# A decoder layer's linear attention: denominators turned to reciprocals on a folded tile and spread by DMA

## What is computed

```
qkv = x @ w_qkv
q_proj = _elu1(jnp.einsum('bhnd,hdf->bhnf', q, proj_matrix))
k_proj = _elu1(jnp.einsum('bhnd,hdf->bhnf', k, proj_matrix))
kv = jnp.einsum('bhnf,bhnd->bhfd', k_proj, v)
attn = jnp.einsum('bhnf,bhfd->bhnd', q_proj, kv)
k_sum = k_proj.sum(axis=2)
z = 1.0 / (jnp.einsum('bhnf,bhf->bhn', q_proj, k_sum) + 1e-08)
attn = attn * z[..., None]
return out @ w_out + b_out      # out: attn with its heads side by side
```

## Time and profile before

| | us |
|---|---|
| median of 3 runs | 2382.08 |
| all three | 2378.66, 2382.08, 2383.08 |
| the profiled execution | 2380.94 |
| its span, first to last instruction | 2379.2 |
| TensorE busy in the span | 2278.0 (96%) |
| VectorE busy | 1390.5 (58%) |
| ScalarE busy | 1158.5 (49%) |
| GpSimd busy | 838.9 (35%) |

### The profile page before, as it was taken

The page is one execution under the profiler, slowest core; times in us unless marked ns, Lnnn a source line. Parts: engine busy times, 40 slices in busy tenths (PEclk is TensorE's granted clock), DMA queues, the critical chain, the costliest instruction groups (busy, mean ns, idle before and its releaser), DMA issues.

```text
span 2379.2 us, 34267 instructions
## 1 busy us (share of the span) xinstructions
PE 2278.0 (96%) x12200; PEld 1775.7 (75%) x12200; DVE 1390.5 (58%) x2258; ACT 1158.5 (49%) x2745; POOL 838.9 (35%) x820
## 2 busy tenths in 40 slices
PE   7999999899998899998799999999999999999998
PEld 6888886566666566665588878888788887888887
DVE  5555456777774668777644466444664445644444
ACT  3555566767663767774544444333343333433332
POOL 1444345333341245545677762111111111111111
PEclk9999999999999899999899999999999999999999
DMA  7655546666646457784656546454345543464442
GB/s 209 161 146 128 134 107 157 210 187 195 177 142 181 102 145 188 185 225 138 217 174 212 177 141 214 171 177 142 129 153 201 177 142 125 136 215 139 140 139 77
DMA packets 140218, 387.46 MB, mean 163 GB/s; under 512 B 15920, under 2 KB 38064, under 8 KB 123440
## 3 DMA queue, kind: packets, MB, share of 16 engines
q1 hardware_dynamic: 139760, 384.77, 53.9%
q10 hardware_dynamic: 288, 0.49, 0.1%
HBM read 254.00 MB, written 104.07 MB: 151 GB/s over the span
## 4 chain that ended last, share of the span: by engine, by line
PE 51%; DVE 1%; issue 0%; ACT 0%; DVEq 0%
PE ex_pg L2593 32%; PE ex_pd L2609 18%; DVE ex_xb L2410 0%; PE ex_pd L2559 0%; PE ex_pd L2570 0%; DVE ex_up L2430 0%; DVE ex_acc L2447 0%; ACT ex_xb L2260 0%; DVE stage L2406 0%; DVE ex_ht L2439 0%; DVE ex_lg L2348 0%; DVE ex_rank L2382 0%; DVE ex_gt L2379 0%; DVE ex_rank L2380 0%; DVE ex_g L2423 0%
## 5 line engine op out<-in xcount | busy, mean ns | idle before, releaser
L2593 PE MATMUL ex_pg<-ex_xb,first_wg 128*128 128x512 f32 x3360 | 821.5, 391 | 12.0 <-DVE ex_up L2430 7.0
L2593 PEld LDWEIGHTS ex_pg<-ex_xb,first_wg 128*128 128x128 f32 x3360 | 632.0, 189 | 153.0 <-issue 15.7
L2609 PE MATMUL ex_pd<-ex_wd,ex_ht 128*128 128x512 f32 x1920 | 486.4, 389 | 2.9 <-issue 2.6
L2609 PEld LDWEIGHTS ex_pd<-ex_wd,ex_ht 128*128 128x128 f32 x1920 | 360.0, 188 | 79.1 <-issue 4.5
L2447 DVE SCALAR_TENSOR_TENSOR ex_acc<-ex_pd,ex_share,ex_acc 128x512 f32<-128x512 f32 x320 | 239.7, 749 | 302.4 <-PE ex_pd L2609 302.2
L2267 ACT COPY ex_m<-ex_pg 128x512 f32<-128x512 f32 x240 | 141.1, 588 | 383.5 <-PE ex_pg L2593 383.4
L2211 POOL TENSOR_TENSOR ex_h<-ex_g,ex_up 128x512 f32<-128x512 f32 x80 | 103.3, 1292 | 553.3 <-issue 458.2
L1590 ACT ACTIVATE cr_prob<-cr_s_bank,cr_top 128x154 f32<-128x154 f32 x512 | 194.7, 401 | 89.3 <-DVE cr_top L1700 86.6
L422 POOL TENSOR_TENSOR pr_ks_sum<-pr_ks_sum,pr_kp 128x512 f32<-128x512 f32 x128 | 165.2, 1291 | 161.6 <-DVE pr_kp L570 150.0
L2271 ACT ACTIVATE ex_g<-ex_g 128x512 f32<-128x512 f32 x160 | 101.3, 633 | 238.0 <-DVE ex_g L2423 165.5
L2203 POOL TENSOR_TENSOR ex_wd<-stage,ex_wd 128x512 fp32r<-128x512 f32 x80 | 105.8, 1343 | 260.1 <-ACT ex_wd L2248 260.1
(11 more groups left out here) (222 smaller groups left out, 3588.9 us busy)
## 6 DMA issues: line engine op xcount, KB each, us to landing
first_wg<-w_scratch SPq DMA_DIRECT2D x60, 1024.0 KB, 5.1
first_wg<-w_scratch SPq DMA_DIRECT2D x60, 768.0 KB, 4.3
w_scratch<-first_wg SPq DMA_DIRECT2D x20, 1792.0 KB, 6.8
stage<-in_units SPq DMA_DIRECT2D x60, 512.0 KB, 6.9
qk<-pr_kq SPq DMA_DIRECT2D x192, 128.0 KB, 2.4
qk<-q_scratch SPq DMA_DIRECT2D x96, 256.0 KB, 4.7
cr_q<-xq_scratch SPq DMA_DIRECT2D x96, 256.0 KB, 8.0
q_scratch<-pr_kq SPq DMA_DIRECT2D x128, 128.0 KB, 2.3
```

The costliest lines, as they stand in the source:

```text
L2593: mm = nc.tensor.matmul(pg[f][BANK[j]][:], wg[:, f, j, s, c * P:(c + 1) * P], xb[:, j, m, c * TB:(c + 1) * TB], start=(k == 0 and j in FRESH),
L2609: mm = nc.tensor.matmul(bank_of("D", n, i)[:], ht[:, s, f, k, t * P:(t + 1) * P], wd[:, n % 2, m, f * D:(f + 1) * D], start=(at == 0), sto ...
```

## The change

The spreading by TensorE goes, with its constant, its banks, the split of the reciprocals on ScalarE and GpSimd. Instead SyncE stores the 16 rows of den to DRAM in four DMAs, loads them back as a tile of 128x64, VectorE takes one reciprocal of that, SyncE stores it back and loads it in four broadcasts to a tile rec of 128x4x512 in fp32, and VectorE multiplies from there. `fold_sums` stands first in SyncE's slot 0, `spread_rec` first in slot 1, each with its waits; the query stores follow in slots 1 to 4 (before: 1, 2, 3 and 7). The fourth group of queries moves from slot 6 to 3, the product from slot 2 to 3, and the output tiles from slots 3 to 5 to slots 4 to 6, with the work that hangs on them. DRAM scratch for the rows is doubled, so that the cross stage has its own. In the cross stage GpSimd waits for the last query stores before it clears two tiles.

The diff, cut to its core:

```
     PLAN = {
         0: [("ND", 3), ("XQ", 0, 0, 12)],
         1: [("XQ", 1, 0, 12)],
-        2: [("R", 0), ("R", 1), ("R", 2), ("R", 3), ("XQ", 2, 0, 12)],
-        3: [("ND", 0), ("O", 0, 0, 12)],
-        4: [("O", 1, 0, 12), ("O", 2, 0, 6)],
-        5: [("ND", 1), ("O", 2, 6, 12), ("O", 3, 0, 12)],
-        6: [("XQ", 3, 0, 12), ("T", 0), ("T", 1)],
+        2: [("XQ", 2, 0, 12)],
+        3: [("ND", 0), ("XQ", 3, 0, 12)],
+        4: [("O", 0, 0, 12), ("O", 1, 0, 6)],
+        5: [("ND", 1), ("O", 1, 6, 12), ("O", 2, 0, 12)],
+        6: [("O", 3, 0, 12), ("T", 0), ("T", 1)],
         7: [("ND", 2), ("T", 2), ("T", 3)],
...
-        spread = sb("spread", [P, G, P], F32R)
-        rec = sb("rec", [P, 2, TB], F32R)
+        rec = sb("rec", [P, G, TB])
...
+        ROWS = 96
+        FOLD = H * TB // P
+        folded = [den[:, 1, n * FOLD:(n + 1) * FOLD] for n in range(2)]
+
+        def folded_rows(i):
+            return rec_dram[i].rearrange("h (k n) -> (h k) n", n=FOLD)
+
+        TAKEN = {"XQ": xq_taken, "O": o_taken, "T": turn_lo}
...
+                def fold_sums(i):
+
+                    sp.wait_ge(den_set, i + 1)
+                    for j in range(HG):
+                        sp.dma_start(rec_dram[i, j * G:(j + 1) * G], den[j * HD:j * HD + G, 0]).then_inc(row_out, 16)
+                    sp.wait_ge(row_out, ROWS * i + 64)
+                    sp.dma_start(folded[0], folded_rows(i)).then_inc(row_out, 16)
+
+                def spread_rec(i):
+
+                    sp.wait_ge(recip_set, i + 1)
+                    sp.dma_start(folded_rows(i), folded[1]).then_inc(row_out, 16)
+                    sp.wait_ge(row_out, ROWS * (i + 1))
+                    if i:
+                        sp.wait_ge(divided, G * i)
+                    rows = rec_dram[i].rearrange("(j g) t -> j g t", j=HG)
+                    for j in range(HG):
+                        sp.dma_start(rec[j * HD:(j + 1) * HD], rows[j:j + 1].broadcast_to([HD, G, TB])).then_inc(rec_in, 16)
+
                 def slot(i, s, ahead, now, behind):
-                    if behind and s in (1, 2, 3, 7):
-                        query_out(i - 1, (1, 2, 3, 7).index(s))
+                    if now and s == 0:
+                        fold_sums(i)
+                    if now and s == 1:
+                        spread_rec(i)
+                    if behind and s in (1, 2, 3, 4):
+                        query_out(i - 1, s - 1)
...
-                def reciprocal_low(i, n):
-                    cols = slice(n * TB // 2, (n + 1) * TB // 2)
-                    pool.wait_ge(rec_hi, 2 * i + n + 1)
-                    nc.gpsimd.tensor_tensor(rec[:, LO, cols], den[:, 1, cols], rec[:, HI, cols].bitcast(F32),
-                                            ALU.subtract).then_inc(rec_set, 1)
...
                     if i:
-                        act.wait_ge(rec_set, 2 * i)
+                        act.wait_ge(row_out, ROWS * (i - 1) + 64)
                     nc.scalar.activation(den[:, 0], p_den[:], ACT.Identity, bias=tiny[:]).then_inc(den_set, 1)
...
-                def reciprocal_high(i, n):
-                    cols = slice(n * TB // 2, (n + 1) * TB // 2)
-                    act.wait_ge(recip_set, 2 * i + n + 1)
-                    nc.scalar.copy(rec[:, HI, cols], den[:, 1, cols]).then_inc(rec_hi, 1)
 
                 def normalised(i, g):
                     if g == 0:
                         act.wait_ge(o_full, TT * i) if i else None
-                    act.wait_ge(r_taken, G * i + g + 1)
+                    act.wait_ge(divided, G * i + g + 1)
                     nc.scalar.copy(u_att[:, HI, g], num[:, g]).then_inc(norm_hi, 1)
...
-                    if now and s == 0:
-                        reciprocal_high(i, 0)
                     if behind and s == 0:
                         query(i - 1, 0)
-                    if now and s == 1 and not ahead:
-                        reciprocal_high(i, 1)
                     if behind and s == 1:
                         query(i - 1, 1)
-                    if now and s == 2:
+                    if behind and s == 2:
+                        query(i - 1, 2)
+                    if behind and s == 3:
+                        query(i - 1, 3)
+                    if now and s == 3:
                         for g in range(G):
                             normalised(i, g)
-                    if behind and s == 2:
-                        query(i - 1, 2)
                     if (ahead or i == -1) and s in (3, 5):
                         take_num(i + 1, (s - 3) // 2)
-                    if behind and s == 6:
-                        query(i - 1, 3)
                     if now and s == 6:
                         turned(i, 0)
...
-                def reciprocal(i, n):
-                    cols = slice(n * TB // 2, (n + 1) * TB // 2)
-                    dve.wait_ge(den_set, i + 1)
-                    nc.vector.reciprocal(den[:, 1, cols], den[:, 0, cols]).then_inc(recip_set, 1)
+                def reciprocal(i):
+                    dve.wait_ge(row_out, ROWS * i + 80)
+                    nc.vector.reciprocal(folded[1], folded[0]).then_inc(recip_set, 1)
 
                 def normalise(i, g):
                     dve.wait_ge(num_taken, G * i + g + 1)
-                    dve.wait_ge(r_full, G * i + g + 1)
-                    nc.vector.tensor_tensor(num[:, g], num[:, g], bank_of(i, "R", g)[:], ALU.mult).then_inc(r_taken, 1)
+                    dve.wait_ge(rec_in, 16 * HG * (i + 1))
+                    nc.vector.tensor_tensor(num[:, g], num[:, g], rec[:, g], ALU.mult).then_inc(divided, 1)
...
-                    if s == 1 and now:
-                        reciprocal(i, 1)
+                        dve.wait_ge(const_in, 32)
                     if s == 6 and now:
-                        add_out(i, 3)
+                        add_out(i, 2)
                     if s == 2 and behind:
                         query(i - 1, 1)
-                    if s == 2 and now:
-                        normalise(i, 0)
                     first()
                     if s == 1 and behind:
                         query(i - 1, 0)
                     if s == 3 and behind:
                         query(i - 1, 2)
-                    if s == 0 and now:
-                        reciprocal(i, 0)
-                    if s == 2 and now:
+                    if s == 3 and now:
+                        normalise(i, 0)
                         normalise(i, 1)
+                    if s == 4 and behind:
+                        query(i - 1, 3)
+                    if s == 6 and now:
+                        norm(i, 1)
+                    if s == 1 and now:
+                        reciprocal(i)
+                    second()
+                    if s == 3 and now:
                         normalise(i, 2)
+                        normalise(i, 3)
                     if s == 4 and now:
                         add_out(i, 0)
+                    if s == 5 and now:
+                        add_out(i, 1)
+                        norm(i, 0)
                     if s == 6 and now:
                         norm(i, 2)
...
-                    if s == 6 and behind:
-                        query(i - 1, 3)
-                    second()
-                    if s == 2 and now:
-                        normalise(i, 3)
-                    if s == 6 and now:
-                        norm(i, 3)
...
-                    if s in (4, 5) and now:
-                        add_out(i, s - 3)
-                        norm(i, s - 4)
-                    if s in (6, 7) and now:
-                        turned(i, 2 * s - 12)
-                        turned(i, 2 * s - 11)
+                    if s == 6 and now:
+                        add_out(i, 3)
+                        turned(i, 0)
+                        turned(i, 1)
+                        norm(i, 3)
+                    if s == 7 and now:
+                        turned(i, 2)
+                        turned(i, 3)
...
-                def spread_out(i, g):
-                    bank_free((i, "R", g))
-                    if g == 0:
-                        pe.wait_ge(rec_set, 2 * (i + 1))
-                    for s in (HI, LO):
-                        mm = nc.tensor.matmul(bank_of(i, "R", g)[:], spread[:, g], rec[:, s], start=(s == HI),
-                                              stop=(s == LO))
-                    mm.then_inc(r_full, 1)
...
+                for landed in xq_out:
+                    pool.wait_ge(landed, 16 * NB * BLK * G // 2)
```

More of the change, by code:

```diff
@@ L106, in decoder_kernel @@
     x1_dram = nc.dram_tensor("x1_scratch", [NBLK, P, TT * D], F32).ap()
-    rec_dram = nc.dram_tensor("rec_scratch", [NBLK, H, TB], F32).ap()
+    rec_dram = nc.dram_tensor("rec_scratch", [2, NBLK, H, TB], F32).ap()
     xq_dram = nc.dram_tensor("xq_scratch", [NBLK, 2, P, C * TB], F32).ap()
@@ L162, in decoder_kernel @@
```

(22 more changed lines are left out.)

16 lines of the change are left out of this document (4 added, 12 removed).

## The result

The changed kernel takes 2474.32 us (median of 4 runs, 2470.6 to 2476.36), the kernel before 2380.85 (4 runs, 2378.66 to 2383.08): a ratio of 1.0391, 95% interval 1.0373 to 1.0409. It is 93 us slower. Forecast were 2473 us, a range of 2403 to 2505, and a chance of 0.88 for slower.

What follows compares the result with a forecast made beforehand. TensorE, the only full engine, bounds the kernel. Middle block -3.1 + 11.5 + 1.1 + 1.3 = +10.8 us, 65 in six; blocks 1, 0, 7 add 8, 5, 14; all +92 on 2382, about 2473 us, range 2403 to 2505.

Steps and rivals of the forecast that it cites:

- Rows landed: Linear stage, each block: the four row stores land at t = 8.5 us, behind the load of x.
- Fold, reciprocal, store back, spread: Rest of a block's DRAM round trip: 2.0, 0.5, 1.6 and 7.5 us, reciprocals in SBUF at t = 20.1.
- The query store: On SyncE's queue it lies behind the spread and lands at t = 21.7 us; ScalarE's query 2 waits for it.
- rival A: Query store doesn't wait for the spread, only the product is late: +4.5 to +5 us a block, 2425 us; chance 0.22.
- From there to slot 5: From the query store's landing, through query, product, cast, subtractions and output matmuls, to slot 5: 12.3 us.
- Clock: TensorE's lower clock for the output tiles after a stall: 1.3 us a block, 0 to 2.5.
- handovers: Allowance of some 0.5 us between engines, within the 12.3 us from the query store's landing to slot 5.
- The boundary: Slot 6 loses its filler between the last output tile and the transposes: 1.1 us a block, 0 to 1.5.
- Blocks: Blocks 1 to 6: +10.8 us each, 65 in six; block 1 another +8 for three weight loads queued ahead.
- The ends: First and last block of the linear stage: block 0 +5 us, block 7 +14 us.
- rival B: Round trip hidden, reciprocals there by t = 14.5, only the 3.1 us a block count: 2357 us; chance 0.1.

Runs made afterwards that it cites:

- the first experiment: On the changed kernel, SyncE's store of query group 0 was put ahead of spread_rec in slot 1, nothing else changed; 2443.31 us, ratio 1.0261.

## Why the prediction was right

Its time, its sign and its mechanism came out. By its own steps (t from the block's first head, 630.46 in the block shown):

- *Rows landed:* 8.5 forecast, 8.8 measured; the load of x ahead of them is the reason, shown by the run that moved it.
- *Fold, reciprocal, store back, spread:* 2.0, 0.5, 1.6, 7.5; measured 1.6, 0.55, 1.5, and 7.1 in the one kernel whose VectorE waits for it.
- *The query store:* ScalarE's query 2 at 21.7 forecast, 21.9 measured. That this store waits behind the spread (and so not rival A) is shown: one store moved gives 31 us. ScalarE idled 9 to 10.4 us in blocks 2 to 7, just above the 6 to 9 named, and 18.0 in block 1. Rival A's price was low too: in the kernel with that store moved a middle block takes 45.6 us, 6.1 more than before, where A had 4.5 to 5 and not the wait of query 3.
- *From there to slot 5:* 12.3 forecast, 13.6 measured (652.40 to 665.99), by terms: query to product 3.2 and 3.1; product and cast 1.3 and 1.5; subtractions 5.0 and 5.9; the rest 2.8 and 3.1. The mis-sized term is the subtractions, and with them the product, which was costed at 0.68 us (0.55 to 0.76): the third and fourth took 1.48 and 1.77 beside GpSimd. It was priced by rows in which it reads one operand from PSUM. In the kernel before, the fourth product runs beside the subtractions too (512.22, GpSimd busy from 511.42 to 516.45) and takes 0.68. The Trainium skill, SBUF — State Buffer, section on who interferes with whom, states this case: a VectorE instruction with two SBUF inputs contends with a GpSimd instruction that reads SBUF. The prediction missed this rule. The trace agrees on who contends. The page has the later one wait out the other, and the times fit that: the third product is recorded from 657.34, the first subtraction runs to 658.27, and the product ends at 658.82, 0.55 us behind it; the second subtraction, recorded from 658.23, takes 1.73 us in place of 1.27. Four subtractions and two products in turn would be 4 x 1.25 + 2 x 0.6 = 6.2 us; it was 5.9.
- *Clock:* 1.3 us a block, kept apart in the sum. From the end of the last subtraction to slot 5 it is 3.1 us here, with a granted clock of 0.71; in the run without the trip and with the high parts first it is 2.2 (613.53 to 615.76), at 1.00. So the clock cost 0.9 us on the path. 12.3 + 1.3 is 13.6, the measured sum, and that is partly luck: GpSimd's 0.9 us were not in it, while 0.5 for handovers was too much and the clock's term 0.4 too large.
- *The boundary:* 1.1 forecast, 0.9 measured; the order alone gave 8.4 us for eight blocks.
- *Blocks:* +10.8 a middle block forecast, +10.6 measured (50.1 against 39.5, blocks 2 to 6). Block 1: +19 forecast, +20 measured (57.7 against 37.7).
- *The ends:* here the sum was lucky. Block 0, up to its store of x1, cost 12 us where +5 was forecast (2.9 of them are the new order, by the run with it alone); block 7, from the store of x1 of block 6 to the cross stage, cost 10 where +14 was. In block 0 slot 5 came at 454.79 and not 451.5: the four subtractions took 7.9 us beside products and a split of the weights on VectorE that also has two SBUF inputs (L1144), against 5.0. With 73 us in blocks 1 to 6 (73 forecast) the stage lost 95 where 92 were forecast, and the cross stage, forecast to be as long as before, gave 4.7 back. So +92 met +93.

Two readings in it are off, without weight in the sum. Its bounds (rows 9.5, fold 3.9, clock 2.5, boundary 1.5) put the high end of a middle block at +15.3, not 14. And a second instruction of the stage did wait for a transfer: VectorE 3.8 us for the bias, once, at the start.

Wrong was **rival B**. It said that with the round trip hidden only the 3.1 us a block count, 2357 us. The run without the trip took 2406, and 2398 with ScalarE's order mended. 8 us of that are the order, which the forecast's sum had and B's left out. Beyond them, the step that failed is "it needs the reciprocals by t = 14.5": that would have helped a product in slot 2, and the change has it in slot 3, behind query 2 on VectorE and with the high parts behind query 3 on ScalarE. So the change's one gain on TensorE's path could not be had in this order, and the chance of 0.1 for B was too much.

## What to carry to other kernels

Before replacing work on a full engine by a transfer, write down the queue's order and ask who waits for the transfers issued *behind* the new ones; here one store that stood in the queue already cost a third of the loss, and the next one behind it kept ScalarE waiting when the first was moved. Then take the new transfer as free and read the block again: if the lead of the work that TensorE needs (5.0 us in the kernel before, 8.4 in the new order with the products in slot 2, 1.4 with them in slot 3, against 5 needed) is gone, no tuning of the transfer brings the gain. An operand that moves from PSUM to SBUF changes the price of an instruction when GpSimd works beside it.

## What was new about the hardware

- VectorE's 128x512 float32 product with both inputs in SBUF took 0.68 us alone and 1.6 (3.17 for two) beside GpSimd's subtractions, which read SBUF; those took 1.25 each alone (4.99 for four), and 1.73 where a product ran beside one. With one input in PSUM the product took 0.68 beside them.
- Two runs with the same matmuls and nearly the same waits for GpSimd differ in how these are spread: in 10 waits (21.5 us in all) TensorE was busy 310.3 us in the stage at a granted clock of 0.92, in 25 waits (20.4 us) 304.6 at 0.95. No run changed the spread of the waits and nothing else.
- A store back of 32 KB, issued 1.9 us behind a store of 512 KB, let its waiter go in 1.5 us (626.26 to 627.72 in the first experiment), whereas row stores of 8 KB issued 1 us behind a load of 1 MB took 6.1. In this kernel a large load ahead held small stores up far more than a store of half its size did; which of size and direction it is, no run here tells apart.
